# The gcn stage's weighted one-hot product in float32, against three bf16 parts of the message and a bf16 one-hot

## The reference, cut to what matters

```python
def _L1_gnn_ref(x, edge_index, edge_weight, W_conv, b_conv, W_lin, b_lin):
    src, dst = (edge_index[0], edge_index[1])
    ...
    deg = jax.ops.segment_sum(w, dst_f, num_segments=n)
    dinv = jnp.where(deg > 0, jax.lax.rsqrt(deg), 0.0)
    norm = dinv[src_f] * w * dinv[dst_f]
    h = x @ W_conv
    agg = jax.ops.segment_sum(h[src_f] * norm[:, None], dst_f, num_segments=n) + b_conv
    return agg @ W_lin + b_lin
```

## Time and profile before

| | |
|---|---|
| median of three executions | 5624.57 us |
| profiled execution, device time | 5618.81 us |
| its span | 5617.0 us |
| PE busy (share of the span) | 4898.8 us (87%) |
| DVE busy | 2794.0 us (50%) |
| ACT busy | 1428.1 us (25%) |
| POOL busy | 633.4 us (11%) |
| mean granted TensorE clock | 0.961 |

### The profile page before, as it was taken

The page is one execution under the profiler, slowest core; times in us unless marked ns, Lnnn a source line. Parts: engine busy times, 40 slices in busy tenths (PEclk is TensorE's granted clock), DMA queues, the critical chain, the costliest instruction groups (busy, mean ns, idle before and its releaser), DMA issues. The chain is left out here.

```text
span 5617.0 us, 281252 instructions
## 1 busy us (share of the span) xinstructions
PE 4898.8 (87%) x116024; PEld 3206.5 (57%) x117274; DVE 2794.0 (50%) x11344; ACT 1428.1 (25%) x4662; POOL 633.4 (11%) x1073
## 2 busy tenths in 40 slices
PE   8899686999898988888888888888888888868789
PEld 6644343444565446666666666666666666644556
DVE  4500344232554665555555555555555555554524
ACT  0000000012232353333333333333333333322313
POOL 0000283000563110000000000000000000010200
PEclk9999897999999999999999999999999999989878
DMA  0000111167443850000000000000000000001000
GB/s 11 15 30 15 28 41 34 45 219 256 137 120 100 296 146 22 12 11 11 11 12 11 11 11 11 12 11 11 11 12 11 11 11 11 8 27 41 16 32 10
DMA packets 153467, 259.51 MB, mean 46 GB/s; under 512 B 47554, under 2 KB 81480, under 8 KB 149037
## 3 DMA queue, kind: packets, MB, share of 16 engines
q1 hardware_dynamic: 98344, 176.13, 9.4%
q0 software_dynamic: 55040, 82.30, 5.1%
HBM read 172.87 MB, written 85.14 MB: 46 GB/s over the span
## 5 line engine op out<-in xcount | busy, mean ns | idle before, releaser
L1558 PE MATMUL bank<-lstm_w,step_h_parts 128*32 128x128 f16 x94848 | 1558.0, 220 | 101.6 <-issue 5.5
L1558 PEld LDWEIGHTS bank<-lstm_w,step_h_parts 128*32 128x32 f16 x94848 | 1341.1, 97 | 451.8 <-issue 300.3
L1630 DVE TRANSPOSE_TENSOR_REDUCE step_summed<-bank 128x4 f32 (+1 forms) x2500 | 792.0, 317 | 1061.1 <-PE bank L1558 895.7
L1553 PE MATMUL bank<-step_xg,step_rows 128*128 (+1 forms) x1252 | 476.0, 381 | 277.9 <-issue 258.2
L1526 ACT ACTIVATE step_act_out<-step_summed,lstm_inv_scale 128x4 f32<-128x4 f32 x625 | 185.8, 297 | 1707.9 <-DVE step_summed L1630 1707.9
L1514 POOL COPY xnT<-step_state 128x4 f32 (+1 forms) x625 | 116.4, 186 | 2743.9 <-DVE step_state L1655 2743.9
L1179 PE MATMUL bank<-sum_parts,sum_hot 125*125 125x512 f16 x1600 | 348.0, 381 | 6.6 <-DVE sum_parts L1138 6.6
L1179 PEld LDWEIGHTS bank<-sum_parts,sum_hot 125*125 125x125 f16 x1600 | 219.8, 137 | 135.2 <-DVE sum_parts L1138 7.7
L1429 PE MATMUL bank<-xg_w,xnT 128*125 128x512 f32 x640 | 277.1, 596 | 6.6 <-DMA xg_w<-in_c_w_ih 6.6
L538 POOL DMA_INDIRECT gcn_rows<-gcn_h_rows,gcn_idx x160 | 202.0, 1262 | 698.6 <-issue 698.3
L1553 PEld LDWEIGHTS bank<-step_xg,step_rows 128*128 128x128 bf16 x2500 | 142.7, 98 | 210.1 <-issue 131.1
(11 more groups left out here) (364 smaller groups left out, 6289.8 us busy)
## 6 DMA issues: line engine op xcount, KB each, us to landing
rel_h<-rel_h_sb SPq DMA_DIRECT2D x39, 1024.0 KB, 6.4
lstm_xg<-cnt POOLq DMA_DIRECT2D x80, 375.0 KB, 4.3
step_xg<-lstm_xg SPq DMA_DIRECT2D x375, 80.0 KB, 2.4
xg_w<-in_c_w_ih SPq DMA_DIRECT2D x16, 1024.0 KB
lstm_w<-in_c_w_hh SPq DMA_DIRECT2D x16, 1024.0 KB, 12.6
cheb_w<-in_L_gnn_weight SPq DMA_DIRECT2D x8, 1024.0 KB
choose_we<-in_L_ffn_experts SPq DMA_DIRECT2D x8, 1024.0 KB
rel_bases<-in_L_gnn_bases SPq DMA_DIRECT2D x8, 1024.0 KB, 11.1
```

The costliest lines, as they stand in the source:

```text
L1553: return nc.tensor.matmul(bank[:], rows[:, p, :], xg[:, at, :], start=True, stop=stop)
L1558: last = nc.tensor.matmul(bank[32 * q:32 * q + 32, 128 * s:128 * s + 128], h_parts[:, c, :], w[:, s, c, q, a, 128 * p:128 * p + 128], star ...
L1630: nc.vector.tensor_reduce(summed[:, 4 * p:4 * p + 4], bank[:, bass.ds(s * 128, 128)].rearrange("p (b r) -> p b r", r=32), X_AXIS, ALU.add, ...
```

## The change

The weight moves from the one-hot to the message. The one-hot becomes a plain 0/1 matrix in bf16. The product m = w * row (float32, 125 by 128) is split into three bf16 parts: hi is m rounded by ACT; rest = m - hi is made by DVE in float32; mid is rest rounded by ACT; lo = rest - mid is made by DVE. TensorE then does three products of bf16 per bank in place of one of float32. `hot`, `rest` and `parts` have four buffers each, and `hot_used` starts at 4. ACT's order is hi of tile k+1, then mid of tile k; it waits for the gather of k+1 before the former. DVE's order is, for each tile: the index copy (one tile in four), rest, one-hot, lo.

```diff
-        hot = sb("gcn_hot", [R, 2, N], F32)
+        hot = sb("gcn_hot", [R, 4, N], BF16)
+        rest = sb("gcn_rest", [R, 4, H], F32)
+        parts = sb("gcn_parts", [R, 4, 3, H], BF16)
...
-            def hots(k, b):
-                nc.vector.tensor_scalar(hot[:, b, :], B.iota_f[:], B.dstf[:, bass.ds(k, 1)],
-                                        B.w[:, bass.ds(k, 1)], ALU.is_equal, ALU.mult).then_inc(hot_ready, 1)
+            def split_rows(k, i):
+                dve.wait_ge(hi_ready, k + 1)
+                nc.vector.scalar_tensor_tensor(out=rest[:, i % 4, :], in0=rows[:, i, :], scalar=B.w[:, bass.ds(k, 1)],
+                                               in1=parts[:, i % 4, 0, :], op0=ALU.mult, op1=ALU.subtract
+                                               ).then_inc(rest_ready, 1)
+                nc.vector.tensor_scalar(hot[:, i % 4, :], B.iota_h[:], B.dstf[:, bass.ds(k, 1)], None,
+                                        ALU.is_equal).then_inc(hot_ready, 1)
+                dve.wait_ge(mid_ready, k + 1)
+                nc.vector.tensor_tensor(parts[:, i % 4, 2, :], rest[:, i % 4, :], parts[:, i % 4, 1, :], ALU.subtract
+                                        ).then_inc(lo_ready, 1)
...
-                    k = g * SLOTS + i
+                    k = dve.snap(g * SLOTS + i)
...
-                    hots(k, i % 2)
+                    split_rows(k, i)
...
+            def keep_hi(k, i, due, at):
+                act.wait_ge(hot_used, k + 1)
+                act.wait_ge(gathered[i], due)
+                nc.scalar.activation(parts[:, i % 4, 0, :], rows[:, i, :], ACT.Copy, scale=B.w[:, at]
+                                     ).then_inc(hi_ready, 1)
+
+            def keep_mid(k, i):
+                act.wait_ge(rest_ready, k + 1)
+                nc.scalar.copy(parts[:, i % 4, 1, :], rest[:, i % 4, :]).then_inc(mid_ready, 1)
+
+            keep_hi(0, 0, 16, slice(0, 1))
+            with act.Fori(0, ET // SLOTS - 1) as g:
+                for i in range(SLOTS):
+                    k = act.snap(g * SLOTS + i)
+                    after = act.snap(k + 1)
+                    keep_hi(after, (i + 1) % SLOTS, act.snap((g + 1 + (i + 1) // SLOTS) * 16), bass.ds(after, 1))
+                    keep_mid(k, i)
...
-            last.then_inc(hot_used, 2)
+            last.then_inc(hot_used, 4)
...
-                    pe.wait_ge(gathered[i], (g + 1) * 16)
                     pe.wait_ge(hot_ready, g * SLOTS + i + 1)
-                    nc.tensor.matmul(B.bank[0][0:H, 0:500], rows[:, i, :], hot[:, i % 2, 0:500], start=False,
-                                     stop=False)
-                    nc.tensor.matmul(B.bank[1][0:H, 0:R], rows[:, i, :], hot[:, i % 2, 500:N], start=False,
-                                     stop=False).then_inc(hot_used, 1)
+                    pe.wait_ge(lo_ready, g * SLOTS + i + 1)
+                    for a in range(3):
+                        nc.tensor.matmul(B.bank[0][0:H, 0:500], parts[:, i % 4, a, :], hot[:, i % 4, 0:500],
+                                         start=False, stop=False)
+                        last = nc.tensor.matmul(B.bank[1][0:H, 0:R], parts[:, i % 4, a, :], hot[:, i % 4, 500:N],
+                                                start=False, stop=False)
+                    last.then_inc(hot_used, 1)
```

More of the change, by code:

```diff
@@ L493, in sem @@
         return nc.alloc_semaphore(name)
[L495 to L498, removed]
+    (loaded, deg_step, root_done, rsqrt_step, h_done, h_scaled, h_stored, idx_kept, hi_ready, rest_ready,
+     mid_ready, lo_ready, hot_ready, hot_used, agg_done, agg_kept, bias_ready, bias_done, out_done) = [sem("gcn_" + n) for n in (
+         "loaded deg_step root_done rsqrt_step h_done h_scaled h_stored idx_kept hi_ready rest_ready "
+         "mid_ready lo_ready hot_ready hot_used agg_done agg_kept bias_ready bias_done out_done").split()]
     gathered = [sem(f"gcn_gathered{i}") for i in range(SLOTS)]
@@ L595, in _ @@
             nc.scalar.activation(root[:], deg[:], ACT.Sqrt).then_inc(root_done, 1)
+            def keep_hi(k, i, due, at):
[13 more added lines that the diff above has]
+                    keep_mid(k, i)
+            for i in range(SLOTS):
+                k = ET - SLOTS + i
+                if i + 1 < SLOTS:
+                    keep_hi(k + 1, i + 1, 16 * (ET // SLOTS), slice(k + 1, k + 2))
+                keep_mid(k, i)
         @block.tensor
```

## The result

The changed kernel takes 5656.8 us (median of five, 5652.19 to 5662.52) against 5624.57; the ratio is 1.0058, 95% interval 1.0043 to 1.0072. That is 32 us slower, where 5623.9 was forecast and 5641 was the upper end of the range. The time is not lost where the change was made.

The account below looks back on a forecast made before the run. POOL's gathers were taken to bound the gcn edge loop. Their pace gives -2.7 us and the loop's end +2.0, in sum -0.7, laid on the median 5624.57 for 5623.9 us; range 5616 to 5641.

Parts of the forecast that it names:

- Sum: -2.7 + 2.0 = -0.7 us: Whole kernel: gcn edge loop's faster gathers, -2.7 us, plus its later end, +2.0 us, against the profiled execution.
- What bounds the loop: Gcn edge loop: POOL's gathers set the pace, before and after; PE, ACT and DVE work is hidden beside them.
- The gathers' pace: Gcn edge loop: 1.55 us a tile after the change against 1.567 before, -2.7 us over 159 steps.
- d: Gcn edge loop: delay of each gather by DVE's work, between 0 and 0.09 us, taken as 0.04.
- The durations: Gcn edge loop, per tile: hi 0.41 us, mid 0.30, rest 0.29, lo 0.29, one-hot 0.39.
- The index copies: Gcn edge loop: DVE's copies reach POOL with 7.5 us of slack, so POOL does not wait for them.
- The end of the loop: Gcn edge loop's end: last product starts 3.03 us after the last landing, 1.05 before; +2.0 us.
- Rival A: Gcn gathers on POOL: each starts under lo or rest and is delayed; pace 1.66 us, 5641 us; chance 0.09.
- rival B: Gcn loop on DVE: its ring of waits or its list outlasts a gather; 1.74 us a tile, 5654 us; chance 0.07.
- rival C: Gcn loop on PE: granted clock falls from 2.4 to 1.2 GHz; six products up to 1.65 us, 5640 us; chance 0.05.
- rival D: Gcn loop: PE, not POOL, sets the pace, so it falls to 1.30 us a tile; 5584 us; chance 0.04.
- the list of what could show it wrong: Gcn loop: wrong if gathers' pace is above 1.63 or below 1.50, or POOL waits over a few us for indices.

Follow-up runs that it names:

- experiment 1: Kernel before the change with 60 empty drain instructions added to VectorE's list in the first block: 5652.64 us, ratio 1.0056.
- experiment 4: Changed kernel with VectorE's LSTM loop aligned to the start of a 256-instruction stretch, first instruction in slot 1: 5623.05 us, ratio 1.0005.
- experiment 9: Changed kernel, loop left where it lies, with product fc moved behind the third reduce in VectorE's LSTM step: 5620.65 us, ratio 0.9998.
- a_head0: Same run as experiment 4: changed kernel, VectorE's LSTM loop aligned to slot 1 of a 256-instruction stretch; 5623.05 us, ratio 1.0005.
- a_head100: Changed kernel with VectorE's LSTM loop aligned to slot 101, across the middle of a 256-instruction stretch: 5628.68 us, ratio 1.0005.
- a_head230: Changed kernel with VectorE's LSTM loop aligned to slot 231, across the end of a 256-instruction stretch: 5659.88 us, ratio 1.0062.
- b_dve60: Same run as experiment 1: kernel before the change with 60 empty drains added to VectorE's list; 5652.64 us, ratio 1.0056.
- a_unroll7: Changed kernel with VectorE's LSTM loop written out seven steps to a round, at the start of a 256-instruction stretch: 5624.69 us, ratio 0.9997.

## Why the prediction was wrong

The forecast was a sum over the gcn stage alone. The step that failed is the one that isn't written down: "Sum: -2.7 + 2.0 = -0.7 us against the profiled execution's 5618.81" lets every other stage keep its time. The LSTM did not: +33.8 us, and the runs show that 60 DVE instructions ahead of it bring 22.3 us of that with the old gcn stage (experiment 1), that placing its loop takes all of it back with the new one (experiment 4), and that taking fc out of the third reduce's way does so too (experiment 9).

Point by point:

- What bounds the loop: right. ACT takes over the wait for the gathers, all 160 of them.
- The gathers' pace: 1.551, predicted 1.55; -2.6 us for -2.7. The longest was 1.38 after the first one; before it was 1.41. The pattern of rest straddling a gather's start is there. That d is small was right; that it is 0.04 rather than 0 or 0.09 was chosen, and that it came true was luck.
- The durations: hi 401 ns for 410, mid 281 for 300, lo 292 for 290, one-hot 388 for 390. Rest was 353 for 290, over the bound of 330: its row had two float32 inputs, and this one has float32 and bf16. It was hidden.
- The index copies: no stall worth the name, 0.3 us at most.
- The end of the loop: 2.73 us from landing to last product for 3.03, so +1.7 for +2.0.
- Rival A (gathers held) would have shown a pace of 1.66, rival B (DVE's ring) 1.74, rival C a low clock, rival D a pace of 1.30. None is in the trace. B's 5654 us is near the measured time by chance: it named another place.

The prediction said that it would be wrong if the gathers' pace left 1.50 to 1.63. It stayed inside and the prediction was wrong all the same: the list of what could show it wrong looked at one stage. In the LSTM, DVE entered its loop 0.141 us later and began its first reduce 0.124 later, so waits that were there before took up 17 ns of it on the mean. A loop of 623 rounds that hangs on so little is a stage to price, whether or not its source is edited.

The Trainium skill, "Runtime: NRT & Kernel Launch", section "Instruction fetch mechanics", says that instructions come in blocks of 256 and that a taken branch out of the two blocks at hand stalls for a fetch. A stall of that kind may be what the directive's own jump shows, once ahead of the loop: from its branch to the next instruction 3.07 us in a_head0 and 3.10 in a_head100, but 0.57 in a_head230. The loops' branches cost far less, 0.10 to 0.14 us more than the shortest, and that rule of the Trainium skill would give them nothing extra: 31 instructions across one end lie in two blocks, and across a middle (a_head100) in one. So that the extra time is a fetch is not shown, and no record of the profile is of one. What the runs do show is that the place decides, and that an end and a middle of a stretch of 256 both count.

Open: what makes the branch long across an end or a middle, why it is 0.33 us in the changed kernel and 0.29 in the two placed ones, and why b_dve60 and the changed kernel differ by 18 ns a step. Of the executions of the kernel before that these comparisons brought, two were some 36 us under the rest (5586.24 and 5586.58 us); they have no profile, and nothing here explains them.

## What to carry to other kernels

An edit that changes how many instructions an engine has moves every loop behind it on that engine. Compare all stages by marks before explaining a difference by the stage edited, and test the placement alone by adding as many empty instructions to the old kernel. Ahead of such an edit, look for long loops in which an engine's entry has no slack, and either place them (here the start of a stretch was the one of three places that cost nothing) or put the instruction that a late entry delays behind the one that sets the pace.

## What the runs showed of the hardware

- A loop-closing branch on VectorE reached the loop's first instruction 0.19 us after its own start when the loop was placed at slot 1 of a stretch of 256 (a_head0), 0.29 us across the middle (a_head100, a_unroll7), 0.29 us across the end (a_head230), and 0.33 us in the changed kernel.
- With the loop across the end, an instruction inside it was late too: 0.153 us after the one before it and not 0.080 (a_head230).
- With 79 and 132 instructions more ahead of TensorE's and ScalarE's LSTM loops the time did not change: 1.0001 [0.9992, 1.0011]. Other places of these loops were not tried.
- An operation of VectorE with two SBUF inputs that was running when an indirect gather started delayed the gather by about its end minus 0.13 us, as in the relational loop: rest ended 0.18 after the start, the gather took 1.27 for 1.21.
